# Language-model tower on one core: GpSimd makes the low part of the output weight, and the Fourier update's deltas become stacked float32r products

## The chip, the core and the metric

The kernel is one program on one NeuronCore of a Trainium2 chip. The metric is the device time of one execution in microseconds (us). Engines are named as in the profile: PE is TensorE (PEld its weight loads), DVE is VectorE, ACT is ScalarE, POOL is GpSimd, SP is SyncE, whose queue (SPq) issues almost all DMAs here.

## What is computed

For 2 x 2048 tokens of width 1024:

```python
h = tok_b + sum_k table_k[token at t-3+k]                  # 4 gathered rows
h = h + attention(layernorm(h))                            # 32 heads, 8 kv heads, head 32, causal, RoPE; then @ w_o.T + b_o
base   = x @ W_base.T + b_base                             # x = layernorm(h)
e      = x @ enc.T                                         # enc: 40 rows (32 + 8)
w      = sum_e coefs_e * mask_e                            # [1024, 40]
update = irfft(e @ w.T)                                    # a fixed 1024x1024 orthogonal matrix F
h = h + base + 0.5 * update
```

The kernel folds the update into the weight of the last layer: W1 = W_base.T + enc.T @ (0.5 * w.T @ F). The 40 x 1024 matrix in brackets is called tw in the code; enc.T @ tw, in eight pieces of 128 rows, are the deltas.

## The kernel before

It has three parts, run one after another. Part A (to about 674 us of the span) gathers tokens, normalises and makes queries, keys and values, which go to DRAM as a float32r high part and a low part. Part B (about 676 to 2800 us) is attention without w_o. Part C is the two last matrix products with their layer norm.

Part B works through 16 groups of four heads. Each group has 36 score steps (a 256-query column block c by a 256-key block i, causal) and 164 maxima entries: an entry is one matmul of up to 128 x 512 scores into one of three PSUM banks (L979, with a mask matmul L982 on the diagonal), and one DVE reduction (L918) that gives the row maxima and frees the bank. PE may be three entries ahead of DVE. The maxima run 14 to 18 steps ahead of the scores. A score step is scores (PE, L1017) into PSUM, exp on ACT (L876), and three steps later (LAG) the product with the values on PE (L1035). The softmax denominators are a product with ones (L1052) of a sum of probabilities that POOL adds up first: the 36 steps are put into 20 sets (set_sum, L850 to L858), each set one denominators product. Every order is written out by hand; each engine runs its list strictly in order, and semaphores hold it.

Two other jobs lie inside part B:

- The output weight w_o. In groups 2 to 9 one 128-row piece per group is loaded (w_raw). ACT rounds each half of it to float32r (w0_hi, L888, at steps 8 and 10), and DVE subtracts that from the piece to get the low part (w0_lo, L946, at steps 12 and 14).
- The Fourier update. Before the first scores, PE gives the 66 entries of steps 0 to 13 (`upfront`). Between them stand eight `fourier(c)` (L1087: two float32 matmuls that add up tw in PSUM) and then eight `delta(c)` (L1098: two float32 matmuls, 40 rows deep, into alternating score banks). ACT scales tw (L901) and copies each delta to SBUF (L904), POOL adds it to a base piece (L820), and SP stores the piece (L809). Eight of ten entries after the last delta are what is left of the 66; two belong to step 0 of group 0, whose scores follow.

Of the kernel before, what the change touches and what calls it, by code (L numbers as in the profile page):

```python
# [17 lines left out]
P = 128  # L18
# [548 lines left out]
SET_OF = [j for j, steps in enumerate(SETS) for s in steps]  # L567
LEAD, FIRST_LEAD = 18, 14
TURN_AFTER = 5
FOUR_AT, DELTA_AT = 8, 36  # L570
W_O_GROUP, DEN_GROUP, DEN_PARTS = 2, 11, 8
DEN_COLS = SEQ * HEADS // P // DEN_PARTS
W_IN, EARLY_W1 = 3, 3
# [39 lines left out]
def part_b(nc, hand, w0_hi, w0_lo, q_hi, q_lo, k_hi, k_lo, v_dram, o_dram, den_dram, recip_dram, w_o_t, w_base_t,  # L613
           w1_dram, enc, fourier_t):

    with ExitStack() as ctx:
# [11 lines left out]
        w_raw = sb("w_raw", [P, D], F32)  # L628
        den = w_raw[:, 0:SEQ * HEADS // P]
        with ExitStack() as early:  # L630
            enc_sb, tw = (early.enter_context(nc.sbuf_tensor(n, [R, D], F32)) for n in ("enc_sb", "tw"))
        probs = sb("probs", [P, SLOTS, 2, GROUP, QW], F32)
        sums = sb("sums", [P, SUM_SLOTS, GROUP, QW], F32)
        od_sb = sb("od_sb", [P, 2, 2, QW], F32)
# [9 lines left out]
        v_loaded = [sem(f"v_loaded{c}") for c in range(QC)]  # L644
        ones_done, k_ones_done = sem("ones_done"), sem("k_ones_done")
        enc_in, base_in = sem("enc_in"), [sem(f"base_in{c}") for c in range(DC)]
        tw_ready, tw_done = sem("tw_ready"), sem("tw_done")
        delta_ready, delta_taken = sem("delta_ready"), sem("delta_taken")
        w1_ready, w1_stored = sem("w1_ready"), sem("w1_stored")
        w_raw_in, w0_hi_done, w0_lo_done = sem("w_raw_in"), sem("w0_hi_done"), sem("w0_lo_done")  # L650
# [15 lines left out]
        def _(sp):  # L666
# [54 lines left out]
            def group(g, first, last):  # L721
# [62 lines left out]
                next_v(2)  # L784
                next_v(3)

            for c in range(FOUR_EARLY, DC):
                sp.dma_start(hand.four[c][:], fourier_t[c * P:(c + 1) * P, :]).then_inc(four_in[c], 16)
            sp.dma_start(enc_sb[:], enc).then_inc(enc_in, 16)
            load_q(0, 2)  # L790
            for c in range(2):
                load_base(c)
            for t in range(TPC):
                sp.wait_ge(hand.v_stored[t], 16 * CHUNKS)
            for s in range(2):
# [1 line left out]
            for c in range(QC):  # L797
                load_k(k_score, 0, c, k_score_loaded)
                load_v(0, c)
            for c in range(2, 4):  # L800
                load_base(c)
            load_q(0, 3)
            send_rows(0, 0)
            for c in range(4, DC):
                load_base(c)
            send_rows(0, 1)
            for c in range(DC):
# [5 lines left out]
        @block.gpsimd  # L813
        def _(pool):
            nc.gpsimd.memset(k_score[M_ROW:P, :].bitcast(F32), 1.0).then_inc(k_ones_done, 1)
            pool.wait_ge(k_ones_done, 1)
            for c in range(DC):
                pool.wait_ge(base_in[c], 16)
                pool.wait_ge(delta_taken, c + 1)
                nc.gpsimd.tensor_tensor(hand.base[:, c, :], hand.base[:, c, :], hand.four[c][:], ALU.add  # L820
                                        ).then_inc(w1_ready, 1)

            for t in range(TPC):
                pool.wait_ge(hand.v_stored[t], 16 * CHUNKS)
            for s in range(2):
                pool.wait_ge(hand.rot_stored[s], 16 * CHUNKS * QK_TILES)
            step = Steps(pool, sum_step, 0)

            def probs_of(g, s, k, lo):
                return probs[:, (g * NS + s) % SLOTS, k, :, lo:QW]  # L830

            def exp_waited(g, s, k):
                pool.wait_ge(exp_done, 2 * (g * NS + s) + k + 1)

            def set_sum(g, j):

                q = g * len(SETS) + j
                at = sums[:, q % SUM_SLOTS]
                diagonal = [s for s in SETS[j] if STEPS[s][0] == STEPS[s][1]]
                wide = [(s, k) for s in SETS[j] for k in range(2) if k == 0 or s not in diagonal]  # L840
                if q >= SUM_SLOTS:
                    g_old, j_old = divmod(q - SUM_SLOTS, len(SETS))
                    pool.wait_ge(batch_done, g_old * NS + SETS[j_old][-1] + 1)
                if len(wide) == 1:
                    exp_waited(g, diagonal[0], 1)
                    nc.gpsimd.tensor_tensor(at[:, :, P:QW], probs_of(g, diagonal[0], 0, P),
                                            probs_of(g, diagonal[0], 1, P), ALU.add).then_inc(sum_done, 1)
                    return
                exp_waited(g, *wide[1])
                step.do(nc.gpsimd.tensor_tensor(at, probs_of(g, *wide[0], 0), probs_of(g, *wide[1], 0), ALU.add))  # L850
                exp_waited(g, *wide[2])
                step.do(nc.gpsimd.tensor_tensor(at, at, probs_of(g, *wide[2], 0), ALU.add))  # L852
                if diagonal:
                    lo, last = P, (diagonal[0], 1)
                else:
                    lo, last = 0, wide[3]
                exp_waited(g, *last)
                nc.gpsimd.tensor_tensor(at[:, :, lo:QW], at[:, :, lo:QW], probs_of(g, *last, lo), ALU.add  # L858
                                        ).then_inc(sum_done, 1)

            for g in range(GROUPS):
                for j in range(len(SETS)):
                    set_sum(g, j)

        @block.scalar
        def _(act):

            def exps(g, s, half):
                c, i = STEPS[s]
                n, lo = g * NS + s, P if i == c and half == 1 else 0  # L870
                act.wait_ge(st_ready, 2 * n + half + 1)
                if half == 0 and n >= SLOTS:
                    g_old, s_old = divmod(n - SLOTS, NS)
                    act.wait_ge(batch_done, n - SLOTS + 1)
                    act.wait_ge(sum_done, g_old * len(SETS) + SET_OF[s_old] + 1)
                nc.scalar.activation(probs[:, n % SLOTS, half, :, lo:QW], st_ps[:, half, :, lo:QW], ACT.Exp,  # L876
                                     scale=float(HD) ** -0.5).then_inc(exp_done, 1)

            def take(g, c):
                act.wait_ge(batch_done, g * NS + LAST_OF[c] + 1)  # L880
                if g * QH + c >= 2:
                    act.wait_ge(stored[c % 2], STORE * (g * (QH // 2) + c // 2))
                nc.scalar.copy(od_sb[:, c % 2], od_ps[:]).then_inc(od_copied, 1)

            def weight_high(c, n):
                cols = slice(n * 512, (n + 1) * 512)
                act.wait_ge(w_raw_in, 16 * (c + 1))
                nc.scalar.copy(w0_hi[:, c, cols], w_raw[:, cols]).then_inc(w0_hi_done, 1)  # L888

            def group(g, first, last):  # L890
                for s in range(NS):
                    k = s - LAG - 1
                    if k % NS in LAST_OF and not (first and k < 0):
                        take(g if k >= 0 else g - 1, LAST_OF.index(k % NS))
                    for half in range(2):
                        exps(g, s, half)
                    if 0 <= g - W_O_GROUP < DC and s in (8, 10):
                        weight_high(g - W_O_GROUP, (8, 10).index(s))

            act.wait_ge(tw_ready, DC)  # L900
            nc.scalar.activation(tw[:], slot_ps[0][0:R, :], ACT.Identity, scale=SCALING).then_inc(tw_done, 1)  # L901
            for c in range(DC):
                act.wait_ge(delta_ready, c + 1)
                nc.scalar.copy(hand.four[c][:], slot_ps[(c + 1) % 2]).then_inc(delta_taken, 1)  # L904
            groups(group)
            take(GROUPS - 1, QH - 1)

        @block.vector
        def _(dve):
# [30 lines left out]
                else:  # L940
                    maxima_rows(g, n, which)

            def weight_low(c, n):
                cols = slice(n * 512, (n + 1) * 512)
                dve.wait_ge(w0_hi_done, 2 * c + n + 1)
                nc.vector.tensor_tensor(w0_lo[:, c, cols], w_raw[:, cols], w0_hi[:, c, cols].bitcast(F32), ALU.subtract  # L946
                                        ).then_inc(w0_lo_done, 1)

            def group(g, first, last):
                for s in range(NS):  # L950
                    for more, n in entries_in(s, first, last):
                        take(g + more, n)
                    if 0 <= g - W_O_GROUP < DC and s in (12, 14):
                        weight_low(g - W_O_GROUP, (12, 14).index(s))
                    if g == DEN_GROUP + 1 and s % 4 == 3 and s // 4 < DEN_PARTS:
                        part = den[:, s // 4 * DEN_COLS:(s // 4 + 1) * DEN_COLS]
                        dve.wait_ge(den_loaded, 16)
# [8 lines left out]
        def _(pe):  # L966
# [123 lines left out]

            def delta(c):
                if c == 0:
                    pe.wait_ge(enc_in, 16)
                    pe.wait_ge(tw_done, 1)
                if c >= 2:
                    pe.wait_ge(delta_taken, c - 1)
                for n in range(2):
                    mm = nc.tensor.matmul(slot_ps[(c + 1) % 2][:, n * 512:(n + 1) * 512], enc_sb[:, c * P:(c + 1) * P],  # L1098
                                          tw[:, n * 512:(n + 1) * 512], start=True, stop=True)
                mm.then_inc(delta_ready, 1)  # L1100

            upfront = [n for k in range(FIRST_LEAD) for n in AT_STEP[k]]
            for j, n in enumerate(upfront):
                give(0, n)
                for what, at in ((fourier, FOUR_AT), (delta, DELTA_AT)):
                    c, between = divmod(j - at, 3)
                    if between == 0 and 0 <= c < DC:
                        what(c)
            groups(group)
# [344 lines left out]
```

## Time and profile before

| | us |
|---|---|
| median of 3 runs | 3563.59 |
| lowest, highest | 3561.82, 3579.18 |
| profiled execution, its own time | 3567.09 |
| its span | 3565.3 |
| mean granted TensorE clock | 0.978 of full speed |

The profiled execution is 3.5 us above the median of the runs, and its time is 1.8 us above its span. The clock has two levels, 1.2 and 2.4 GHz; a granted clock of 0.50 is the lower, 1.00 the upper.

### The profile page before, as it was taken

How to read it: one execution, taken by the hardware profiler on the slowest of the kernel's cores; microseconds unless marked ns; L12 is line 12 of the kernel's file. 1: busy time of each engine (PE TensorE's matmuls, PEld its weight loads, DVE VectorE, ACT ScalarE, POOL GpSimd, SP SyncE). 2: the span in 40 equal slices, each digit the busy share in tenths (PEclk: the TensorE clock that was granted, in tenths of full speed). 3: DMA queues.
4: the chain of work that ended last, by engine and by line, in shares of the span. 5: the costliest groups of instructions: out<-in, count | busy, mean ns of one | idle time of the engine just before them, and what ended most of it. 6: DMA issues, size and time to landing. Idle time of an engine off the chain costs nothing. (4 is left out here: it accounts for less than half of the span.)

```text
span 3565.3 us, 61290 instructions
## 1 busy us (share of the span) xinstructions
PE 3413.7 (96%) x25088; PEld 2362.2 (66%) x25088; DVE 2288.3 (64%) x3914; ACT 1421.9 (40%) x1677; POOL 2266.6 (64%) x1042
## 2 busy tenths in 40 slices
PE   1999999999999999999999999999999799999999
PEld 1778888646666566566566666666665488888887
DVE  3677777667777777777777777777775344444443
ACT  2222232135555555555555555555555301111010
POOL 4443220159889889889989989998998622222221
PEclk8999999979999999999999999999999899999999
DMA  8999874721221122122122122112212234333332
GB/s 230 248 255 233 238 207 132 208 77 33 57 62 49 43 64 57 36 62 56 38 68 60 28 61 59 45 42 62 50 39 63 83 88 94 93 90 90 94 95 65
DMA packets 248219, 334.59 MB, mean 94 GB/s; under 512 B 64346, under 2 KB 153818, under 8 KB 247938
## 3 DMA queue, kind: packets, MB, share of 16 engines
q1 hardware_dynamic: 229506, 263.54, 27.3%
q0 software_dynamic: 18432, 67.12, 8.8%
q8 instruction: 198, 3.24, 0.4%
q14 instruction: 83, 0.68, 0.1%
HBM read 227.80 MB, written 101.71 MB: 92 GB/s over the span
## 5 line engine op out<-in xcount | busy, mean ns | idle before, releaser
L918 DVE TENSOR_REDUCE mpart<-mx_ps 128x1 f32<-128x512 f32 (+3 forms) x2560 | 1429.6, 604 | 530.1 <-PE mx_ps L982 342.6
L876 ACT ACTIVATE probs<-st_ps 128x1024 f32<-128x1024 f32 (+1 forms) x1152 | 1063.9, 974 | 828.2 <-PE st_ps L1017 642.7
L979 PE MATMUL mx_ps<-k_max,qs 96*128 96x512 f32 (+3 forms) x2560 | 907.5, 415 | 16.3 <-DVE mpart L918 12.3
L1017 PE MATMUL st_ps<-qs,k_score 98*128 98x512 f32 (+1 forms) x2304 | 719.9, 407 | 0.2
L850 POOL TENSOR_TENSOR sums<-probs 128x1024 f32<-128x1024 f32 x256 | 610.1, 2383 | 160.4 <-ACT probs L876 160.4
L979 PEld LDWEIGHTS mx_ps<-k_max,qs 96*128 96x128 f32 x2560 | 463.9, 194 | 313.1 <-DVE mpart L918 206.1
L852 POOL TENSOR_TENSOR sums<-sums,probs 128x1024 f32<-128x1024 f32 x256 | 609.7, 2381 | 37.8 <-ACT probs L876 19.9
L1035 PE MATMUL od_ps<-probs,vs 128*32 128x256 f32 (+1 forms) x9216 | 595.3, 376 | 0.0
L858 POOL TENSOR_TENSOR sums<-sums,probs 128x1024 f32<-128x1024 f32 (+1 forms) x256 | 543.8, 2124 | 20.3 <-ACT probs L876 0.3
L1017 PEld LDWEIGHTS st_ps<-qs,k_score 98*128 98x128 f32 x2304 | 421.3, 194 | 72.6 <-ACT probs L876 12.3
L1210 POOL TENSOR_TENSOR h<-h,bb 128x1024 f32<-128x1024 f32 x32 | 104.1, 3254 | 509.1 <-DVE xn_c L1284 509.1
L1035 PEld LDWEIGHTS od_ps<-probs,vs 128*32 128x32 f32 x9216 | 242.5, 110 | 229.8 <-issue 116.7
L291 POOL DMA_INDIRECT hbuf<-in_tok_table,idx_all x128 | 193.8, 1514 | 307.2 <-DMA hbuf<-in_tok_table,idx_all 162.5
L491 PE MATMUL qk_ps<-x_hi,w_hi 128*128 128x512 f32 x640 | 254.3, 397 | 17.0 <-ACT rotation L343 14.7
L491 PE MATMUL qk_ps<-x_lo,w_hi 128*128 128x512 f32 x640 | 251.4, 393 | 0.0
L491 PE MATMUL qk_ps<-x_hi,w_lo 128*128 128x512 f32 x640 | 251.4, 393 | 0.0
L982 PE MATMUL mx_ps<-masks 128*128 128x128 bf16 x1024 | 238.0, 234 | 0.0
L1272 DVE TENSOR_TENSOR h<-oc_ps,h_in 128x1024 f32<-128x1024 f32 x31 | 38.0, 1224 | 256.3 <-PE oc_ps L1325 256.3
L1052 PE MATMUL od_ps<-sums,ones 128*32 128x256 f32 (+1 forms) x2560 | 186.0, 363 | 16.1 <-POOL sums L858 16.1
L982 PEld LDWEIGHTS mx_ps<-masks 128*128 128x128 bf16 x1024 | 100.8, 98 | 103.0 <-issue 60.1
L1237 ACT ACTIVATE std_c<-var_c 128x1 f32<-128x1 f32 x32 | 6.5, 203 | 405.2 <-DVE var_c L1279 405.2
L1325 PE MATMUL f_ps<-w_hi,xc_hi 128*128 128x512 f32 x512 | 158.9, 392 | 6.4 <-DVE xc_lo L1294 6.4
(108 smaller groups left out, 4076.5 us busy)
## 6 DMA issues: line engine op xcount, KB each, us to landing
qs<-q_hi_scratch SPq DMA_DIRECT2D x128, 256.0 KB, 4.8
h_scratch<-hbuf SPq DMA_DIRECT2D x32, 512.0 KB, 8.3
q_hi_scratch<-rot_hi SPq DMA_DIRECT2D x64, 256.0 KB, 4.0
q_lo_scratch<-rot_lo SPq DMA_DIRECT2D x64, 256.0 KB, 4.7
qs<-q_lo_scratch SPq DMA_DIRECT2D x64, 256.0 KB, 5.8
o_scratch<-od_sb SPq DMA_DIRECT2D x128, 128.0 KB
o_in<-o_scratch SPq DMA_DIRECT2D x32, 512.0 KB, 5.0
o_in<-recip_scratch SPq DMA_DIRECT2D x128, 128.0 KB, 8.1
```

Source lines behind the costliest of these rows:

```text
L291: nc.gpsimd.indirect_dma_start(hbuf[:, m % 2, t, :], None, tables[k], bass.IndirectOffsetOnAxis(ap=idx[:, m, j:j + 1], axis=0), compute_op ...
L491: mm = nc.tensor.matmul(qk_ps[:, f % 2, :], w[a], x[b], start=(c == 0 and k == 0), stop=(c == DC - 1 and k == 2))
L850: step.do(nc.gpsimd.tensor_tensor(at, probs_of(g, *wide[0], 0), probs_of(g, *wide[1], 0), ALU.add))
L852: step.do(nc.gpsimd.tensor_tensor(at, at, probs_of(g, *wide[2], 0), ALU.add))
L858: nc.gpsimd.tensor_tensor(at[:, :, lo:QW], at[:, :, lo:QW], probs_of(g, *last, lo), ALU.add).then_inc(sum_done, 1)
L876: nc.scalar.activation(probs[:, n % SLOTS, half, :, lo:QW], st_ps[:, half, :, lo:QW], ACT.Exp, scale=float(HD) ** -0.5).then_inc(exp_done, 1)
L918: nc.vector.tensor_reduce(mpart[:, h * TPC + t, kc:kc + 1], mx_ps[:, e % MAX_BANKS, 0:w], AX, ALU.max).then_inc(max_done, 1)
L979: mm = nc.tensor.matmul(out, qs[c][0:K_ROWS, h, t * P:(t + 1) * P], k_max[0:K_ROWS, kc * CT:kc * CT + w], start=True, stop=not diagonal)
L982: mm = nc.tensor.matmul(out[:, w - P:w], ident_m, mqk, start=False, stop=True)
L1017: mm = nc.tensor.matmul(out[:, :, lo:QW], k_score[0:M_ROW + 2, kt * P:(kt + 1) * P], qs[c // 2][0:M_ROW + 2, h:h + 2, at + lo:at + QW], st ...
L1035: mm = nc.tensor.matmul(od_ps[h * HD:(h + 1) * HD, 0, lo:QW], vs[:, 2 * i + k, :], probs[:, n % SLOTS, k, h, lo:QW], start=s in FIRST_OF a ...
L1052: mm = nc.tensor.matmul(od_ps[h * HD:(h + 1) * HD, 1, lo:QW], ones[:], sums[:, q % SUM_SLOTS, h, lo:QW], start=False, stop=s in LAST_OF)
```

## The change

1. `weight_low` leaves DVE's list and enters POOL's, with the same 16 operations (128 x 512, two SBUF inputs), now after sets 7 and 10 of a group.
2. `delta` uses float32r. The exact float32 product of two 40-row operands is replaced by one float32r product 120 rows deep: enc3 holds high, high and low rows of enc, and tw3 high, low and high rows of tw. The low parts are made on POOL (enc_lo, tw_lo), the high parts on ACT, and four small DMAs on SP's queue (`rows_sent`) copy the second and third 40 rows to their partitions.
3. A fourier stands after every second entry from entry 8 (before: every third), so the last is at entry 22 (before: 29). A delta stands after every entry from entry 50 (before: every third from 36). The last delta is at entry 57 in both.
4. On SP's queue enc is loaded first, one base piece is loaded early and seven after the tw rows.

```diff
-FOUR_AT, DELTA_AT = 8, 36
+FOUR_AT, FOUR_EVERY, DELTA_AT, DELTA_EVERY = 8, 2, 50, 1
@@ SP
+            def rows_sent(dst, row, src, sent):
+                sp.dma_start(dst[row:row + R].bitcast(F32), src[0:R].bitcast(F32)).then_inc(sent, 16)
+
+            sp.dma_start(enc_sb[:], enc).then_inc(enc_in, 16)
             for c in range(FOUR_EARLY, DC):
                 sp.dma_start(hand.four[c][:], fourier_t[c * P:(c + 1) * P, :]).then_inc(four_in[c], 16)
-            sp.dma_start(enc_sb[:], enc).then_inc(enc_in, 16)
             load_q(0, 2)
-            for c in range(2):
-                load_base(c)
+            sp.wait_ge(enc_hi_done, 1)
+            rows_sent(enc3, R, enc3, enc_rows)
+            sp.wait_ge(enc_lo_done, 1)
+            rows_sent(enc3, 2 * R, enc_lo, enc_rows)
+            load_base(0)
...
-            for c in range(2, 4):
-                load_base(c)
             load_q(0, 3)
             send_rows(0, 0)
-            for c in range(4, DC):
+            sp.wait_ge(tw_hi_done, 1)
+            rows_sent(tw3, 2 * R, tw3, tw_rows)
+            sp.wait_ge(tw_lo_done, 1)
+            rows_sent(tw3, R, tw_lo, tw_rows)
+            for c in range(1, DC):
                 load_base(c)
@@ POOL
+            nc.gpsimd.tensor_tensor(enc_lo[:], enc_sb[:], enc3[0:R].bitcast(F32), ALU.subtract).then_inc(enc_lo_done, 1)
...
+            nc.gpsimd.tensor_tensor(tw_lo[:], tw[:], tw3[0:R].bitcast(F32), ALU.subtract).then_inc(tw_lo_done, 1)
...
+            def weight_low(c, n):
+                cols = slice(n * 512, (n + 1) * 512)
+                pool.wait_ge(w0_hi_done, 2 * c + n + 1)
+                nc.gpsimd.tensor_tensor(w0_lo[:, c, cols], w_raw[:, cols], w0_hi[:, c, cols].bitcast(F32), ALU.subtract
+                                        ).then_inc(w0_lo_done, 1)
+
             for g in range(GROUPS):
                 for j in range(len(SETS)):
                     set_sum(g, j)
+                    if 0 <= g - W_O_GROUP < DC and j in (7, 10):
+                        weight_low(g - W_O_GROUP, (7, 10).index(j))
@@ ACT
+            act.wait_ge(enc_in, 16)
+            nc.scalar.copy(enc3[0:R], enc_sb[:]).then_inc(enc_hi_done, 1)
             act.wait_ge(tw_ready, DC)
+            nc.scalar.activation(tw3[0:R], slot_ps[0][0:R, :], ACT.Identity, scale=SCALING).then_inc(tw_hi_done, 1)
             nc.scalar.activation(tw[:], slot_ps[0][0:R, :], ACT.Identity, scale=SCALING).then_inc(tw_done, 1)
@@ DVE
-            def weight_low(c, n):
...
-                    if 0 <= g - W_O_GROUP < DC and s in (12, 14):
-                        weight_low(g - W_O_GROUP, (12, 14).index(s))
@@ PE
                 if c == 0:
-                    pe.wait_ge(enc_in, 16)
-                    pe.wait_ge(tw_done, 1)
+                    pe.wait_ge(enc_rows, 32)
+                    pe.wait_ge(tw_rows, 32)
...
-                    mm = nc.tensor.matmul(slot_ps[(c + 1) % 2][:, n * 512:(n + 1) * 512], enc_sb[:, c * P:(c + 1) * P],
-                                          tw[:, n * 512:(n + 1) * 512], start=True, stop=True)
+                    mm = nc.tensor.matmul(slot_ps[(c + 1) % 2][:, n * 512:(n + 1) * 512], enc3[:, c * P:(c + 1) * P],
+                                          tw3[:, n * 512:(n + 1) * 512], start=True, stop=True)
...
-                for what, at in ((fourier, FOUR_AT), (delta, DELTA_AT)):
-                    c, between = divmod(j - at, 3)
+                for what, at, every in ((fourier, FOUR_AT, FOUR_EVERY), (delta, DELTA_AT, DELTA_EVERY)):
+                    c, between = divmod(j - at, every)
```

On PE, the end of the upfront list stood like this before (mx_ps rows are maxima entries, L1098 a delta, L1017 the first scores):

```order
L979 MATMUL mx_ps<-k_max,qs 128x512 x3
L1098 MATMUL st_ps<-tw,enc_sb 128x512 x2
L979 MATMUL mx_ps<-k_max,qs 128x512 x2
L987 MATMUL mx_ps<-ident,mcol 16x128
L1098 MATMUL st_ps<-tw,enc_sb 128x512 x2
L979 MATMUL mx_ps<-k_max,qs 128x512 x3
L1098 MATMUL st_ps<-tw,enc_sb 128x512 x2
L979 MATMUL mx_ps<-k_max,qs 128x512 x10
L1017 MATMUL st_ps<-qs,k_score 128x512
```

and stands like this now (L1121 is a delta, L1040 the first scores):

```order
L1121 MATMUL st_ps<-tw,enc 128x512 x2
L1010 MATMUL mx_ps<-ident,mcol 16x128
L1121 MATMUL st_ps<-tw,enc 128x512 x2
L1002 MATMUL mx_ps<-k_max,qs 128x512
L1121 MATMUL st_ps<-tw,enc 128x512 x2
L1002 MATMUL mx_ps<-k_max,qs 128x512
L1121 MATMUL st_ps<-tw,enc 128x512 x2
L1002 MATMUL mx_ps<-k_max,qs 128x512
L1121 MATMUL st_ps<-tw,enc 128x512 x2
L1002 MATMUL mx_ps<-k_max,qs 128x512 x10
L1040 MATMUL st_ps<-qs,k_score 128x512
```

The deltas have one entry between them where they had three, and the ten entries behind the last one are the same. Ahead of them, 28 entries now follow the last fourier without any other product.

On DVE, in group 2, the two low parts stood between reductions of step 12 to 14 (x41 and x9 are reductions in a row):

```order
L931 TENSOR_SCALAR m_hi<-mx_ps 16x128
L933 SCALAR_TENSOR_TENSOR m_lo<-mx_ps,m_hi 16x128
L918 TENSOR_REDUCE mpart<-mx_ps 128x1 x41
L946 TENSOR_TENSOR w_lo<-w_raw,w_hi 128x512
L918 TENSOR_REDUCE mpart<-mx_ps 128x1 x9
L946 TENSOR_TENSOR w_lo<-w_raw,w_hi 128x512
L918 TENSOR_REDUCE mpart<-mx_ps 128x1 x9
L922 TENSOR_REDUCE mcol<-mpart 128x16
```

On POOL in the same group they now stand behind the sums of sets 7 and 10 (each set is three additions, L870 to L878):

```order
L878 TENSOR_TENSOR sums<-sums,probs 128x1024
L884 TENSOR_TENSOR w_lo<-w_raw,w_hi 128x512
L870 TENSOR_TENSOR sums<-probs 128x1024
L872 TENSOR_TENSOR sums<-sums,probs 128x1024
L878 TENSOR_TENSOR sums<-sums,probs 128x1024
L870 TENSOR_TENSOR sums<-probs 128x1024
L872 TENSOR_TENSOR sums<-sums,probs 128x1024
L878 TENSOR_TENSOR sums<-sums,probs 128x4x128
L870 TENSOR_TENSOR sums<-probs 128x1024
L872 TENSOR_TENSOR sums<-sums,probs 128x1024
L878 TENSOR_TENSOR sums<-sums,probs 128x1024
L884 TENSOR_TENSOR w_lo<-w_raw,w_hi 128x512
```

DVE's list in a group with a weight piece is now the same as in one without; POOL's is longer by two operations.

## Rows read from the trace of the kernel before

**Rows 1.** The page: span, and busy time of the engines.

```profile
span 3565.3 us, 61290 instructions
PE 3413.7 (96%) x25088; PEld 2362.2 (66%) x25088; DVE 2288.3 (64%) x3914; ACT 1421.9 (40%) x1677; POOL 2266.6 (64%) x1042
```

**Rows 2.** Timeline of ACT, copies of finished column blocks: start us, us, engine, line.

```profile
1029.13 0.59 ACT L883 COPY od_sb<-od_ps 128x512 f32<-128x512 f32 x1 [0.93 <-PE od_ps L1052]
...
1316.68 0.59 ACT L883 COPY od_sb<-od_ps 128x512 f32<-128x512 f32 x1 [0.45 <-PE od_ps L1052]
1337.34 0.59 ACT L883 COPY od_sb<-od_ps 128x512 f32<-128x512 f32 x1
...
2064.20 0.59 ACT L883 COPY od_sb<-od_ps 128x512 f32<-128x512 f32 x1 [0.93 <-PE od_ps L1052]
2190.20 0.59 ACT L883 COPY od_sb<-od_ps 128x512 f32<-128x512 f32 x1 [0.93 <-PE od_ps L1052]
...
2221.28 0.59 ACT L883 COPY od_sb<-od_ps 128x512 f32<-128x512 f32 x1 [0.45 <-PE od_ps L1052]
2238.10 0.59 ACT L883 COPY od_sb<-od_ps 128x512 f32<-128x512 f32 x1
```

**Rows 3.** Instructions of L946: duration ns min/median/max, first and last start us.

```profile
L946 DVE TENSOR_TENSOR w_lo<-w_raw,w_hi x16: 2416/2603/2769, 1059.7 to 1974.3; 128x512 fp32r<-128x512 f32 x16
```

**Rows 4.** Timeline of DVE, POOL and ACT, group 2; first row part A.

```profile
672.79 0.68 DVE L433 TENSOR_TENSOR rot_lo<-rotation,rot_hi 128x512 fp32r<-128x512 f32 x1
...
1059.73 2.42 DVE L946 TENSOR_TENSOR w_lo<-w_raw,w_hi 128x512 fp32r<-128x512 f32 x1
...
1059.22 2.38 POOL L852 TENSOR_TENSOR sums<-sums,probs 128x1024 f32<-128x1024 f32 x1
...
1052.17 0.62 ACT L888 CAST w_hi<-w_raw 128x512 fp32r<-128x512 f32 x1
```

**Rows 5.** Timeline of POOL and PE, group 11 (no weight piece).

```profile
2234.45 2.38 POOL L850 TENSOR_TENSOR sums<-probs 128x1024 f32<-128x1024 f32 x1 [2.11 <-ACT probs L876]
...
2252.79 2.39 POOL L858 TENSOR_TENSOR sums<-sums,probs 128x1024 f32<-128x1024 f32 x1
...
2258.81 0.61 PE L1052 MATMUL od_ps<-sums,ones 128*32 128x256 f32 x8
```

**Rows 6.** Timeline of PE, start of part B.

```profile
679.42 3.17 PE L1087 MATMUL st_ps<-four,wr 128*40 128x512 f32 x4
...
694.11 0.72 PE L979 MATMUL mx_ps<-k_max,qs 96*128 96x512 f32 x2
694.76 1.91 PE L1087 MATMUL st_ps<-four,wr 128*40 128x512 f32 x4
...
742.26 3.78 PE L1098 MATMUL st_ps<-tw,enc_sb 40*128 40x512 f32 x4
745.97 5.95 PE L979 MATMUL mx_ps<-k_max,qs 96*128 96x512 f32 x10
751.72 0.63 PE L1017 MATMUL st_ps<-qs,k_score 98*128 98x512 f32 x1
...
768.01 0.40 PE L1052 MATMUL od_ps<-sums,ones 128*32 128x128 f32 x8
```

**Rows 7.** Windows: stretch, length, busy PE, PEld, DVE, ACT, POOL, then clock, DMA share.

```profile
706.00:760.00 54.00, 54.00 (x99) 23.33 (x97) 22.56 (x40) 12.63 (x13) 20.01 (x9) 0.50 0.34 123
```

**Rows 8.** Timeline of DVE, ACT, POOL, start of part B.

```profile
746.80 6.07 DVE L918 TENSOR_REDUCE mpart<-mx_ps 128x1 f32<-128x512 f32 x10 [3.40 <-PE mx_ps L979]
...
702.17 1.02 ACT L901 ACTIVATE tw<-st_ps 40x1024 f32<-40x1024 f32 x1 [29.58 <-PE st_ps L1087]
...
747.23 2.36 POOL L820 TENSOR_TENSOR base<-base,four 128x1024 f32<-128x1024 f32 x1 [2.95 <-ACT four L904]
...
755.39 1.27 POOL L846 TENSOR_TENSOR sums<-probs 128x512 f32<-128x512 f32 x1 [5.80 <-ACT probs L876]
```

**Rows 9.** Instructions on base: landing of its DMAs, eight loads and eight stores.

```profile
DMA to landing us min/median/max: 2.9/5.0/15.2
```

More of the change, by code:

```diff
@@ L630, in part_b @@
         with ExitStack() as early:
-            enc_sb, tw = (early.enter_context(nc.sbuf_tensor(n, [R, D], F32)) for n in ("enc_sb", "tw"))
+            held = lambda n, rows, d: early.enter_context(nc.sbuf_tensor(n, [rows, D], d))
+            enc_sb, tw = held("enc_sb", R, F32), held("tw", R, F32)
+            enc_lo, tw_lo = held("enc_lo", R, F32R), held("tw_lo", R, F32R)
+            enc3, tw3 = held("enc3", 3 * R, F32R), held("tw3", 3 * R, F32R)
         probs = sb("probs", [P, SLOTS, 2, GROUP, QW], F32)
@@ L646, in part_b @@
         enc_in, base_in = sem("enc_in"), [sem(f"base_in{c}") for c in range(DC)]
-        tw_ready, tw_done = sem("tw_ready"), sem("tw_done")
+        enc_hi_done, enc_lo_done, enc_rows = sem("enc_hi_done"), sem("enc_lo_done"), sem("enc_rows")
+        tw_ready, tw_done, tw_hi_done = sem("tw_ready"), sem("tw_done"), sem("tw_hi_done")
+        tw_lo_done, tw_rows = sem("tw_lo_done"), sem("tw_rows")
         delta_ready, delta_taken = sem("delta_ready"), sem("delta_taken")
@@ L816, in _ @@
             pool.wait_ge(k_ones_done, 1)
+            pool.wait_ge(enc_hi_done, 1)
+            nc.gpsimd.tensor_tensor(enc_lo[:], enc_sb[:], enc3[0:R].bitcast(F32), ALU.subtract).then_inc(enc_lo_done, 1)
+            pool.wait_ge(enc_lo_done, 1)
+            pool.wait_ge(tw_hi_done, 1)
+            pool.wait_ge(tw_done, 1)
+            nc.gpsimd.tensor_tensor(tw_lo[:], tw[:], tw3[0:R].bitcast(F32), ALU.subtract).then_inc(tw_lo_done, 1)
+            pool.wait_ge(tw_lo_done, 1)
             for c in range(DC):
@@ L941, in take @@
                     maxima_rows(g, n, which)
-            def weight_low(c, n):
[L944 to L947, printed above, removed]
             def group(g, first, last):
```

## The prediction

> **What bounds the kernel now.** I read the page first: PE is busy for 96% of the span, DVE and POOL for 64% each [rows 1]. PE sets the pace, so an edit is worth what it takes out of PE's waits or off PE's own list, wherever it stands. Two stretches concern the change.
>
> The first is attention. Each group ends its first column block with a copy on ACT, so the distance between two such copies is a group's length. The reader is to see two lengths. From group 2 to group 10 it is 2064.20 - 1029.13 = 1035.07 us for eight groups, 129.4 each; from there to group 11 it is 126.00 [rows 2]. Only groups 2 to 9 hold a weight piece. Inside a group the difference sits in one place: between the copies of blocks 3 and 4 lie 20.66 us in group 4 and 16.82 us in group 11, so 3.84 of it [rows 2]. That is where DVE does its two low parts. Each takes 2.4 to 2.8 us, 16 in all [rows 3], while the same form in part A takes 0.68 [rows 4]. The first of them starts at 1059.73 and ends at 1062.15; POOL's addition, begun at 1059.22, ends at 1061.60 [rows 4]. What is left behind POOL's end is 0.55 us, about the length of the operation. So DVE stands and waits until POOL's instruction is over. Three maxima banks cover 1.8 us of reductions, and PE then stands too.
>
> That wait has a rule in the Trainium skill (SBUF — State Buffer, "Who interferes with whom"): a DVE operation with two SBUF inputs and a GpSimd operation take one shared port pair exclusively, and the later one blocks. The trace agrees: 1061.60 plus 0.55 is DVE's end.
>
> The second stretch is the start of part B, 679.42 (first fourier) to 751.72 (first scores). The last delta ends at 745.97 [rows 6]. PE never rests there, and from 706 to 760 it has the lower clock, 0.50 or 1.2 GHz [rows 7]. A float32 delta takes 3.71 us of it (742.26 to 745.97) [rows 6].
>
> **The weight's low part leaves DVE.** DVE's list in groups 2 to 9 becomes that of group 11, so each should take 126.00: 1035.07 - 8 x 126.00 = **27.1 us** less. ACT's two roundings stay; group 2's second is at 1052.17, before the disputed stretch, and delayed nothing there.
>
> **It enters POOL.** No row shows this form on POOL. The nearest is its addition of 128 x 512, 1.27 us [rows 8]; the upper bound is one of twice the size, 2.39 [rows 5]; the lower is DVE's 0.68 [rows 4]. I take 1.27, the same element count. What does it delay? In group 11 POOL waits 2.11 us for ACT before set 9 [rows 5], so the operation behind set 7 is absorbed there. Behind set 10 there is no such gap at once: set 11 is summed at 2255.18 and PE asks for it at 2258.81, 3.63 us later [rows 5]. 1.27 fits, 2.39 too. Sets 12 to 15 come with the same delay, until the next wait for ACT. Both inputs are old by then (ACT rounds at steps 8 and 10, set 7 ends with step 12). Cost 0; if that cover were gone, 16 x 1.27 = 20 us. SP's next load of w_raw waits for the low parts, but only at the next group's start.
>
> The Trainium skill speaks against this edit (GPSIMD Engine Reference, "Engine selection"): two-input elementwise work belongs on VectorE, GpSimd being about 2x slower. The rows give 1.27 against 0.68, so by engine time alone 16 x 0.59 = 9 us would be lost where I count 27 gained. The traced DVE time, 2.6, is the one that counts here.
>
> **Fouriers closer.** Product and cost stay: the first at the low clock ends at 682.6, each later one takes 1.84 (1.91 less 0.07 overlap), two entries 0.65 [rows 6]. So the last ends at 682.6 + 7 x 2.49 = 700.0, where before ACT began tw at 702.17 [rows 8]: 2.1 us earlier.
>
> **From there to the first delta.** 28 entries, nothing else. DVE sets their pace: 6.07 / 10 = 0.61 for a wide one [rows 8]. The 16 diagonal ones are narrower; before, 28 entries and 8 deltas filled 702.2 to 745.97, so 43.8 - 8 x 3.71 = 14.1, 0.50 an entry. I take 12 x 0.61 + 16 x 0.50 = 15.3, less two entries (1.2) that PE is ahead: first delta at about 714.1.
>
> **Are the tw rows there?** ACT makes tw3 and tw, 1.02 each [rows 8], to 702.1. POOL's tw_lo over 40 x 1024 has no row; its 128 x 1024 operation takes 2.36 [rows 8], and one partition's length is the same: 704.5. Its DMA then lands within 2.9 to 15.2 us, the quickest and slowest on base (stores in an idle queue, loads in a full one), median 5.0 [rows 9]. Only one base load now stands ahead, three fewer, so I take the median: 709.5, with 4.6 us of slack. At 15.2 it is 719.7 and PE waits 5.6. The enc rows go 15 us earlier and cost nothing; SP comes to the key loads about 2 us later, but those keys are first used at the scores. The four loads sit one 160 KB load later; the six had landed well before use and I charge nothing, at most 1 us.
>
> **Deltas.** Each is two matmuls of 512 columns in one float32r pass, at 1.2 GHz 0.43 us each: 0.86 for 3.71. An entry between costs PE 0.43. 8 x 0.86 + 7 x 0.43 = 9.9: the last ends at 724.0. ACT's copy, about as long as tw's 1.02, frees the bank two deltas later, at 2.6 us, so it does not hold. Behind the last delta the same ten entries as before: 751.72 - 745.97 = 5.75. First scores at 729.8, **21.9 us** earlier.
>
> **What is late next.** POOL's eight additions to base, 2.36 each [rows 8], 18.9 in all, now start at about 716.4 and end at 735.3. POOL took up the first sum at 755.39 [rows 8], shifted to 733.5: 1.8 us late. PE asked for it at 768.01 [rows 6], 11.4 us after its end, so nothing waits. SP stands in the stores as long; its next work, group 1's queries, waits for the scores of step 2 anyway.
>
> **Sum.** 27.1 + 21.9 = 49.0. The profiled execution goes from 3567.1 to 3518.1. The median is 3.5 lower than that execution: 3563.6 - 49.0 = **3514.6**.
>
> **The rivals.**
>
> *The rows come late* (or another wait of that size at the first delta). For: four DMAs in a queue whose loads took up to 15.2. Against: 3 base loads fewer ahead. Loses 5.6: 3520. Chance 0.12.
>
> *POOL's operation costs more than its slack.* It must pass 3.6 us behind set 10. At twice the upper bound, 4.8, PE loses 1.2 us, eight times: 10 us, 3524. Chance 0.06.
>
> *It was not the low parts but the rest of the weight work* (ACT's roundings, the load). Then groups stay at 129.4 and only 21.9 comes: 3542. Against it: the delay begins behind block 3's copy. Chance 0.04. If half of each gain is lost by something unseen, 3539, also here.
>
> *Price by engine time* (the rule above): 3563.6 - 21.9 + 9 gives 3551, no change that can be told. As a mechanism: POOL is the bound in the weight groups, and each operation there shows in full. Against it: POOL's 2.11 us wait for ACT. Chance 0.02.
>
> *Slower.* POOL's operation would have to block until PE loses more than is gained: with 3.6 us of slack behind set 10 and 5 behind set 7, 16 operations must take some 49.0 / 16 + 4.3 = 7.4 us each to reach no change, and 8.5 for 0.5% slower, at least three and a half times the upper bound. Chance 0.01.
>
> **How the numbers follow.** Forecast 0.75, 3514.6. Its own spread: the clock. If it rises earlier, because the deltas are dense and 120 rows deep, the deltas and first steps cost up to 7 us less; if it rises later, 3 more. Narrow entries between 0.40 and 0.60 are 1.6 either way. With the late rows and the costlier POOL operation inside, 3506 to 3528. 0.5% (18 us) is about what a measurement of this kernel can tell; the border for faster is 3545.8. Faster 0.96, same 0.03, slower 0.01.
>
> **What would show it.** Right: all 15 distances between group copies at 126.0 (group 0 apart); low parts on POOL at about 1.3 us; no DVE row of 2.4; first scores near 730 and first delta near 714 with no idle time on PE for a DMA. Wrong: a wait of denominators (L1052's counterpart) for POOL sums behind sets 8 or 11; PE idle at the first delta; groups 2 to 9 still longer than 126.

## The result, and the profile after

The changed kernel takes 3514.97 us (median of 4 runs, 3510.39 to 3517.75); beside it the kernel before took 3562.70 (4 runs, 3559.94 to 3579.18). The difference of the medians is 47.7 us. The ratio of the runs is 0.9853, 95% interval 0.9836 to 0.987 (it is not the quotient of the two medians, which is 0.9866): 1.5% faster, at the predicted time and inside its range. The profiled execution took 3517.54 us, with a span of 3515.7, 49.6 less than before.

The page of the changed kernel, busy times:

```profile
PE 3374.0 (96%) x25072; PEld 2349.4 (67%) x25072; DVE 2251.6 (64%) x3898; ACT 1422.5 (40%) x1679; POOL 2289.2 (65%) x1060
```

The shares read as those of before [rows 1]; one cannot see in them where 50 us went. The group lengths can. Timeline of ACT, the copies that answer to [rows 2] (start us, us, engine, line):

```profile
1008.96 0.59 ACT L911 COPY od_sb<-od_ps 128x512 f32<-128x512 f32 x1 [0.93 <-PE od_ps L1075]
...
1292.05 0.59 ACT L911 COPY od_sb<-od_ps 128x512 f32<-128x512 f32 x1 [0.45 <-PE od_ps L1075]
1308.86 0.58 ACT L911 COPY od_sb<-od_ps 128x512 f32<-128x512 f32 x1
...
2016.99 0.59 ACT L911 COPY od_sb<-od_ps 128x512 f32<-128x512 f32 x1 [0.93 <-PE od_ps L1075]
2142.96 0.59 ACT L911 COPY od_sb<-od_ps 128x512 f32<-128x512 f32 x1 [0.93 <-PE od_ps L1075]
```

Groups 2 to 9 take 2016.99 - 1008.96 = 1008.03 us, 126.0 each, like the group after them (125.97). That is 27.04 less than 1035.07. In group 4 the copies of blocks 3 and 4 are 16.81 us apart, where they were 20.66 apart.

The low parts, and POOL's timeline around the first of them in group 2:

```profile
L884 POOL TENSOR_TENSOR w_lo<-w_raw,w_hi x16: 1269/1284/1293, 1043.8 to 1948.7; 128x512 fp32r<-128x512 f32 x16
```

```profile
1043.83 1.29 POOL L884 TENSOR_TENSOR w_lo<-w_raw,w_hi 128x512 fp32r<-128x512 f32 x1
1045.09 2.37 POOL L870 TENSOR_TENSOR sums<-probs 128x1024 f32<-128x1024 f32 x1
...
1053.22 2.38 POOL L870 TENSOR_TENSOR sums<-probs 128x1024 f32<-128x1024 f32 x1 [0.84 <-ACT probs L904]
```

An operation takes 1.28 us on POOL where it took 2.6 on DVE. Before set 9 POOL now waits 0.84 us for ACT, 1.27 less than the 2.11 in [rows 5]: the wait has swallowed the operation.

The other gain is at the start of part B. Timeline of PE (an x8 groups eight instructions that follow each other):

```profile
678.54 0.30 PE L1002 MATMUL mx_ps<-k_max,qs 96*128 96x128 f32 x1 [2.57 <-PEq L158]
...
682.21 3.64 PE L1110 MATMUL st_ps<-four,wr 128*40 128x512 f32 x4
...
701.80 1.91 PE L1110 MATMUL st_ps<-four,wr 128*40 128x512 f32 x4
703.64 0.97 PE L1002 MATMUL mx_ps<-k_max,qs 96*128 96x512 f32 x3
...
718.74 1.05 PE L1121 MATMUL st_ps<-tw,enc 120*128 120x512 f32 x2
719.59 0.63 PE L1002 MATMUL mx_ps<-k_max,qs 96*128 96x512 f32 x1
720.02 1.05 PE L1121 MATMUL st_ps<-tw,enc 120*128 120x512 f32 x2
...
726.46 0.73 PE L1121 MATMUL st_ps<-tw,enc 120*128 120x512 f32 x2
727.03 0.85 PE L1002 MATMUL mx_ps<-k_max,qs 96*128 96x512 f32 x3
...
732.14 0.39 PE L1040 MATMUL st_ps<-qs,k_score 98*128 98x512 f32 x1
```

From the first maxima matmul to the first scores it is 732.14 - 678.54 = 53.6 us; before, the scores at 751.72 [rows 6] stood 75.31 behind their first maxima matmul (676.41). That is 21.7 less. No delta waits for its rows. The granted clock by stretch (the columns of [rows 7]; the clock is the third number from the end):

```profile
710.00:718.00 8.00, 8.00 (x31) 5.41 (x30) 7.13 (x16) 0.00 (x0) 0.00 (x0) 0.50 0.94 353
718.00:726.00 8.00, 7.80 (x22) 5.32 (x23) 5.81 (x12) 5.48 (x6) 4.99 (x3) 0.67 0.29 116
726.00:740.00 14.00, 12.79 (x46) 6.27 (x44) 13.55 (x23) 7.57 (x9) 14.00 (x7) 1.00 0.65 263
...
742.00:746.00 4.00, 4.00 (x18) 2.89 (x17) 1.40 (x5) 1.82 (x2) 3.65 (x3) 0.50 0.53 117
```

It is low when the deltas begin and back at 1.00 before they end; before, it stayed at 0.50 up to 760. But it is low once more from about 740 to 747, behind the first scores. The first copy of a column block stands 16.2 us behind the first scores here. In three of the experiments below that start in the same way, the clock stays at 1.00 in that stretch, and it is 13.7. So about 2.5 us of the start vary between executions of the same order.

The two gains make 48.7 of the span's 49.6. The rest is small differences with both signs: part A 2.1 us longer, the stretch from the first scores to the first copy 0.6 shorter, the last group with part C 2.4 shorter. The change touches neither part A nor part C, and in the other kernels the first maxima matmul stands anywhere from 674.8 to 680.8.

### The profile page after: what moved, and what is told of

Its sections match the earlier page's. It is cut to its first block and busy times, and to the rows that moved or that the text cites. A ratio compares the mean times of both kernels' runs of the same rounds, so it can differ in the third digit from the quotient of the medians.

```text
span 3515.7 us, 61268 instructions
## 1 busy us (share of the span) xinstructions
PE 3374.0 (96%) x25072; PEld 2349.4 (67%) x25072; DVE 2251.6 (64%) x3898; ACT 1422.5 (40%) x1679; POOL 2289.2 (65%) x1060
## 5 line engine op out<-in xcount | busy, mean ns | idle before, releaser
L1040 PE MATMUL st_ps<-qs,k_score 98*128 98x512 f32 (+1 forms) x2304 | 720.4, 408 | 0.2
L870 POOL TENSOR_TENSOR sums<-probs 128x1024 f32<-128x1024 f32 x256 | 609.7, 2382 | 128.8 <-ACT probs L904 128.0
L878 POOL TENSOR_TENSOR sums<-sums,probs 128x1024 f32<-128x1024 f32 (+1 forms) x256 | 538.8, 2105 | 20.3 <-ACT probs L904 0.3
L1040 PEld LDWEIGHTS st_ps<-qs,k_score 98*128 98x128 f32 x2304 | 421.2, 194 | 73.0 <-ACT probs L904 12.4
```

Of the source, the lines that this page charges most:

```text
L1040: mm = nc.tensor.matmul(out[:, :, lo:QW], k_score[0:M_ROW + 2, kt * P:(kt + 1) * P], qs[c // 2][0:M_ROW + 2, h:h + 2, at + lo:at + QW], st ...
```

## The experiments

The theory is that of the prediction: DVE's subtraction waits for the port that it shares with POOL, POOL has room for the work, and the start is what the deltas cost at the low clock. The rivals: the weight groups were long for another reason; POOL has no room; the order of the products, not their form, gave the start. Each kernel is the changed one but for its edit, except the second, which is the kernel before. "Less" is the difference of the medians of the kernel before and of the experiment, on the same chip (three sets of runs; before 3566.84 for the first four, 3568.62 for the next four and 3569.34 for the last two). Group lengths, the start (first maxima matmul to first scores) and the distance from the same matmul to the first copy of a column block are from the profiled execution, in us. In the kernels that have the changed one's order there the start spreads from 52.2 to 53.6 and the first copy from 65.9 to 69.8; in the kernel before they are 75.3 and 92.1.

| kernel | median us | less | ratio (95%) | groups 2 to 9 | start of part B | to the first copy |
|---|---|---|---|---|---|---|
| low part on DVE | 3541.21 | 25.6 | 0.9929 (0.9912 to 0.9945) | 128.2 to 129.9 | 53.3 | 67.0 |
| only the low part moved | 3541.25 | 25.6 | 0.993 (0.9914 to 0.9947) | 126.0 | 76.2 | 95.8 |
| low part twice | 3512.69 | 54.2 | 0.9852 (0.9835 to 0.9868) | 126.0 | 52.2 | 65.9 |
| low part four times | 3572.91 | -6.1 | 1.0013 (1.0004 to 1.0023) | 133.1 to 133.6 | 53.6 | 69.8 |
| DVE reads the piece alone | 3512.96 | 55.7 | 0.9847 (0.983 to 0.9863) | 126.0 to 126.1 | 53.3 | 67.0 |
| float32 deltas | 3542.36 | 26.3 | 0.9932 (0.9915 to 0.9949) | 126.0 to 126.1 | 80.1 | 96.9 |
| old places | 3522.13 | 46.5 | 0.9867 (0.9847 to 0.9888) | 126.0 to 126.1 | 56.6 | 76.2 |
| fouriers every third | 3511.22 | 57.4 | 0.9847 (0.9828 to 0.9867) | 126.0 | 50.2 | 63.9 |
| products spread | 3519.97 | 49.4 | 0.986 (0.9845 to 0.9875) | 126.0 | 54.7 | 69.8 |
| deltas every second | 3512.87 | 56.5 | 0.9837 (0.9824 to 0.9851) | 125.9 to 126.0 | 50.3 | 66.6 |

**The two halves.** The first kernel gives the low part back to DVE, the second makes only that move in the kernel before.

```diff
 # low part on DVE: the changed kernel
-                    if 0 <= g - W_O_GROUP < DC and j in (7, 10):      # POOL
-                        weight_low(g - W_O_GROUP, (7, 10).index(j))
...
+                    if 0 <= g - W_O_GROUP < DC and s in (12, 14):     # DVE
+                        weight_low(g - W_O_GROUP, (12, 14).index(s))
```

The function `weight_low` moves with its calls, and `nc.gpsimd` in it becomes `nc.vector`.

> The changed kernel with the weight's low part back on DVE at steps 12 and 14; the start of part B stays changed. Wait theory (DVE stands until POOL's running instruction is over, PE then runs out of maxima banks): groups 2 and 3 at 128.2, groups 4 to 9 at 129.8 again, 27 us more than the changed kernel, 3542. Rival (the weight groups are long because of ACT's roundings or the load): nothing returns, 3515. Rival (the two parts of the change hide one another): clearly more or less than 27.

> The kernel before with only the move of the low part to POOL. If the two terms simply add: 27 us less than before, 3536, all groups at 126.0 and the start of part B as before (first scores 75.3 us after part B's first matmul). Rival (the terms are coupled, for instance POOL's backlog at the start matters): another number than 27.

In the first the low parts are slow again, with everything else as changed:

```profile
L969 DVE TENSOR_TENSOR w_lo<-w_raw,w_hi x16: 2406/2587/2773, 1036.4 to 1949.8; 128x512 fp32r<-128x512 f32 x16
```

Its weight groups are 128.2 to 129.9, in the second all are 126.0. By ratio the halves give 0.7% each, 1.4% together, against 1.47% for the whole, each with an interval of about 0.17% on either side: within that they add up, and nothing is seen to be given back between them.

**Twice and four times.** POOL repeats the same subtraction.

```diff
+                for k in range(3):                                    # 1 for twice
+                    step.do(nc.gpsimd.tensor_tensor(w0_lo[:, c, cols], w_raw[:, cols], w0_hi[:, c, cols].bitcast(F32),
+                                                    ALU.subtract))
                 nc.gpsimd.tensor_tensor(w0_lo[:, c, cols], w_raw[:, cols], w0_hi[:, c, cols].bitcast(F32), ALU.subtract
                                         ).then_inc(w0_lo_done, 1)
```

> The changed kernel with each low-part operation on POOL made twice (the same values are written twice; 1.28 us more, 1.35 with the hand-over). Slack theory: behind set 10 the changed kernel has 2.39 us left between POOL's sum of set 11 and PE's use. Twice costs about 0.6 behind set 7 after the wait for ACT, and 1.35 behind set 10, so 0.4 us is left: groups stay at 126.0 and the time at 3515. Rival (POOL is the bound in these groups and each operation shows): 16 x 1.35 = 22 us more, 3537.

> The changed kernel with each low-part operation on POOL made four times (same values). Slack theory: 4 x 1.35 = 5.4 us behind set 7, of which some 2.1 is absorbed in POOL's wait for ACT, so 3.3 late at set 9, against a slack of 3.47; then 5.4 more behind set 10 against 3.6: PE waits some 5 us in each of eight groups, about 40 us more, 3555 (30 to 50). POOL-bound rival: 48 x 1.35 = 65 us more, 3580.

Twice costs nothing. Four times costs 7.2 us in each of the eight groups, some 58 in all, where the slacks of the prediction gave 40 (30 to 50): a miss. In size that is nearer to the 65 of the rival by which every operation on POOL shows in full; what speaks against this rival is twice, where it wanted 22 us and none came. Four times, timeline of POOL and of PE in group 3, and PE's denominators in the weight groups (busy us, mean ns, idle before and its releaser):

```profile
1205.58 4.01 POOL L885 TENSOR_TENSOR w_lo<-w_raw,w_hi 128x512 fp32r<-128x512 f32 x3
1209.67 1.28 POOL L887 TENSOR_TENSOR w_lo<-w_raw,w_hi 128x512 fp32r<-128x512 f32 x1
1210.91 2.38 POOL L870 TENSOR_TENSOR sums<-probs 128x1024 f32<-128x1024 f32 x1
...
1218.18 1.08 PE L1078 MATMUL od_ps<-sums,ones 128*32 128x256 f32 x8 [4.31 <-POOL sums L878]
```

```profile
L1078 PE MATMUL od_ps<-sums,ones 128*32 128x256 f32 (+1 forms) x1160 | 86.3, 371 | 31.2 <-POOL sums L878 30.2
```

Two things were missing in my slacks. The two places share one budget: what the operation behind set 7 costs beyond POOL's 2.11 us of waiting is still there behind set 10. So 2 x 5.14 - 2.11 - 3.63 = 4.5 us, and 4.31 is measured; with 5.33, the time from 1205.58 to the next sum at 1210.91, it would be 4.9. For twice, 2 x 2.57 - 5.74 is below zero. And the clock falls with the idle time. The same kernel, windows behind that wait:

```profile
1216.00:1218.00 2.00, 0.00 (x0) 0.00 (x0) 0.00 (x0) 0.00 (x0) 2.00 (x1) 0.75 0.00 0
1218.00:1220.00 2.00, 1.81 (x10) 0.91 (x11) 0.00 (x0) 0.58 (x1) 2.00 (x3) 0.50 0.00 0
1220.00:1222.00 2.00, 2.00 (x6) 1.52 (x6) 1.29 (x2) 0.69 (x1) 1.92 (x2) 0.50 0.20 68
```

31.2 us of waits in the window of 1043 to 2015 are about 4 a group; the other 3 go with PE at 0.50 for some 5 us behind each. That this halving costs 3 is argued from the rows, not tried by itself.

**DVE reads the piece alone.** If DVE waited for its SBUF operands as such, and not for a port that only two inputs need, any DVE operation on the piece at these steps would wait.

```diff
+                    if 0 <= g - W_O_GROUP < DC and s in (12, 14):     # DVE, POOL keeps the low part
+                        half = (12, 14).index(s)
+                        dve.wait_ge(w0_hi_done, 2 * (g - W_O_GROUP) + half + 1)
+                        nc.vector.tensor_reduce(scrap[:], w_raw[:, half * 512:(half + 1) * 512], AX, ALU.max
+                                                ).then_inc(scrap_done, 1)
```

SP's next load of the piece waits for `scrap_done` too (not shown).

> The changed kernel with two more operations on DVE in groups 2 to 9, at steps 12 and 14 where the low parts stood: a maximum over one half of w_raw, 128 x 512 from SBUF, one input, about 0.6 to 0.7 us of engine time, the same as a low part's own. The low parts stay on POOL. Port theory (only a DVE operation with two SBUF inputs waits for POOL's instruction): each shows as 0.6 to 0.7 us, is mostly covered by the three banks, groups at 126.0 to 126.6, at most 5 us in all, 3515 to 3520. Rival (any extra DVE work or any SBUF input there costs the same): DVE rows of 2.4 us and groups at 128 to 130, 3542.

```profile
L985 DVE TENSOR_REDUCE scrap<-w_raw x16: 673/676/677, 1033.6 to 1922.3; 128x1 f32<-128x512 f32 x16
```

Timeline of the same kernel, the first of them and POOL's operation at that time:

```profile
1033.60 0.68 DVE L985 TENSOR_REDUCE scrap<-w_raw 128x1 f32<-128x512 f32 x1
...
1033.05 2.39 POOL L876 TENSOR_TENSOR sums<-sums,probs 128x1024 f32<-128x1024 f32 x1
```

It begins and ends inside POOL's addition and takes 0.68 us; all 16 do. The wait belongs to an operation of DVE with two SBUF inputs while POOL has one that reads SBUF, as the Trainium skill says (SBUF — State Buffer, "Who interferes with whom").

A reduction is not a subtraction: it also writes one column where the subtraction writes 512. Four things support the reading. The two-input form too takes 0.68 while POOL has no addition to make [rows 4]. Before the change all 16 subtractions ended 0.55 or 0.56 us behind the end of POOL's running addition. The next addition of POOL was the longer one then, 2.68 or 2.69 for 2.38, which fits each engine waiting for the other. And a DVE operation that writes 64 columns, but has one SBUF input, does not wait either: the kernel before has eight such reciprocals in group 12, all beside an addition of POOL, at 541 to 545 ns. Kernel before, POOL behind the first low part, and the third reciprocal:

```profile
1061.68 2.68 POOL L858 TENSOR_TENSOR sums<-sums,probs 128x1024 f32<-128x1024 f32 x1
...
2343.89 0.54 DVE L958 RECIPROCAL w_raw<-w_raw 128x64 f32<-128x64 f32 x1
...
2343.82 2.39 POOL L850 TENSOR_TENSOR sums<-probs 128x1024 f32<-128x1024 f32 x1
```

No run has an operation with one input that writes all 512 columns there.

**Float32 deltas.** The stacked operands are still made, but the product is the old one.

```diff
-                    mm = nc.tensor.matmul(slot_ps[(c + 1) % 2][:, n * 512:(n + 1) * 512], enc3[:, c * P:(c + 1) * P],
-                                          tw3[:, n * 512:(n + 1) * 512], start=True, stop=True)
+                    mm = nc.tensor.matmul(slot_ps[(c + 1) % 2][:, n * 512:(n + 1) * 512], enc_sb[:, c * P:(c + 1) * P],
+                                          tw[:, n * 512:(n + 1) * 512], start=True, stop=True)
```

> The changed kernel with float32 deltas, 40 rows deep, at the new places (all preparation of the stacked operands stays and is waited for). Forecast's term: a float32 delta costs 3.7 us at 1.2 GHz against 0.86, so eight cost 23 us more, from 53.6 to about 76 us between part B's first matmul and the first scores, 3538. Rival (the gain came from the places, since the entries between the old deltas were hidden work): a few us only, about 3520. With the clock at 2.4 GHz in the deltas it would be 8 x 1.85 = 15 against 8.7, 6 to 8 us more.

```profile
715.17 3.78 PE L1121 MATMUL st_ps<-tw,enc_sb 40*128 40x512 f32 x4
719.61 3.78 PE L1121 MATMUL st_ps<-tw,enc_sb 40*128 40x512 f32 x4
```

With the new places and the old product the start is 80.1 us, longer than before the change. The form of the product is worth 26.5 us against the changed kernel's start, all of the gain and more; the medians say 29.4 against DVE reads the piece alone, measured beside it (3542.36 and 3512.96). The eight deltas stand 4.43 apart and take 34.3 us where the changed kernel takes 8.3, and the clock is at 0.50 from 706 to 760. How much of this is the shorter product and how much the clock that comes back earlier was not separated; at the low clock alone a delta with its entry takes 4.43 against 1.28.

**The places.** `FOUR_AT, FOUR_EVERY, DELTA_AT, DELTA_EVERY` is 8, 2, 50, 1 in the changed kernel.

```diff
-FOUR_AT, FOUR_EVERY, DELTA_AT, DELTA_EVERY = 8, 2, 50, 1
+FOUR_AT, FOUR_EVERY, DELTA_AT, DELTA_EVERY = 8, 3, 36, 3   # old places
+FOUR_AT, FOUR_EVERY, DELTA_AT, DELTA_EVERY = 8, 3, 50, 1   # fouriers every third
+FOUR_AT, FOUR_EVERY, DELTA_AT, DELTA_EVERY = 2, 3, 40, 2   # products spread
+FOUR_AT, FOUR_EVERY, DELTA_AT, DELTA_EVERY = 8, 3, 44, 2   # deltas every second
```

> The changed kernel with float32r deltas at the old places (fouriers every third entry from 8, deltas every third from 36). The last fourier is at entry 29, six entries before the first delta; the stacked rows land some 8 us after the last fourier, so PE should wait at the first delta for about 5 us, and the rest of the entries are the same work: first scores about 3 us later than in the changed kernel, 3518. Rival (places do not matter): 3515. Rival (the wait also lowers the clock for the deltas and costs more): 3522.

> The changed kernel with the fouriers every third entry (8 to 29) and the deltas still every entry from 50. Three entries take DVE 1.8 us, as long as a fourier takes PE, so DVE's idle time of the changed kernel between fouriers is filled: the last fourier ends 0.6 us later, with 7 entries fewer behind it (4.2 us). 3.6 us less than the changed kernel, 3511, first scores 50 us after part B's first matmul; the stacked rows must land within 21 entries (11 us), which leaves 3. Rival (the rows are late): no gain, 3515.

> Only the numbers that place the products differ from the changed kernel: Fourier products from entry 2 at every third entry, delta products from entry 40 at every second. If the part between the first maxima and the first scores is set by the sum of PE's work and by its clock, the products filling gaps that DVE's reductions leave, this start is 2 to 4 us shorter than the changed kernel's 53.6 us and the time is some 3 us less, hardly to be told from it. If the rows of the second product have to be in place first, as in the kernel with the products at their old places (it waited 4.6 us), PE waits up to 5 us at the first delta and the time is not below that of the changed kernel.

> Fourier products from entry 8 at every third, deltas from entry 44 at every second. The first delta comes some 2.5 us later in the entries than in the kernel with the products spread furthest, so the rows are there and PE waits for none of them; the start is 2 to 4 us shorter than the changed kernel's 53.6 us. If a denser row of deltas is what raises the clock, it stays at the low level here and the start is as long as the changed kernel's or longer.

The first delta at the old places, and then with the products spread:

```profile
714.71 1.19 PE L1121 MATMUL st_ps<-tw,enc 120*128 120x512 f32 x2 [4.56 <-DMA tw<-tw_lo]
```

```profile
713.54 1.19 PE L1121 MATMUL st_ps<-tw,enc 120*128 120x512 f32 x2 [1.99 <-DMA tw<-tw_lo]
```

So the rows can be late, and a later first delta is what hides them. With the old places the cost is larger than this wait. The clock is 0.50 from 714 to 726 and low again behind it (0.57 from 734 to 746), so the first copy comes 9.2 us later than in DVE reads the piece alone, and the medians of these two, measured side by side, are 9.2 apart as well. That is the rival of its expectation by which the wait lowers the clock; that the wait is what lowers it is argued. The rows leave POOL at 711.6 and 707.3 in these two, and land 3.1 and 6.2 us later; with deltas every second it is 3.1 again and a wait of 0.9, where none was expected. The densest fouriers gain nothing: one after every third entry gives the shortest start, 50.2. More entries then stand beside the fouriers: DVE is busy for 8.9 of the 12 us from 690 to 702, in the changed kernel for 5.8. Against the changed kernel's 53.6 that is 3.4 us, against the shortest start of the same order 2.0, and the medians cannot tell them apart (1.7 us less than DVE reads the piece alone beside it; 0.9847 and 0.9853, each interval 0.003 to 0.004 wide). Deltas at every second entry end at the same start, with the clock back at 1.00 as well, so the clock does not need a delta after every entry to come back; there group 0 is 2.8 us longer than in the changed kernel (137.44 against 134.61, at a clock of 0.98), which eats most of the gain in the profiled execution. No version beats the changed kernel by what can be measured.

## Why the prediction was right, step by step

The mechanism of both gains is borne out, but for the closer fouriers. That the time came within 0.4 us of the forecast is luck: the changed kernel's own runs spread over 7 us, two kernels with the same start and the same group lengths (low part twice, DVE reads the piece alone) gave 54.2 and 55.7 us in their sets where 49.0 was forecast, and two errors at the start cancelled (below).

- **The low part leaves DVE, 27.1 us.** Measured 27.04, and shown by both halves. Its mechanism was half of the story: groups 2 and 3 were 2.2 us too long, groups 4 to 9 3.8 (below).
- **It enters POOL at no cost.** Shown, by the groups of 126.0 and by the low part twice. The price of 1.27 was 1.28. The two slacks were used as if they were separate; at this size that did not matter. It did in the rival called slower: its break-even of 7.4 us an operation is wrong, since four operations in a row, about 5.2 us, already end at 1.0013. The rival stood nearer than it was put, but still four times the real price off.
- **Fouriers closer, the last one 2.1 us earlier.** The weakest step. Counted from the first maxima matmul the last fourier ended after 25.1 us, forecast 23.6: the first one ran wholly at the low clock (3.64 us, before 3.17), and the entries around it too. The entries up to the first delta took 15.1 for 14.1; with the clock at 0.50 the widest diagonal ones stand 0.67 us apart, where 0.50 was taken for all 16. Together the first delta is 2.5 us late, and the experiment with the old distance shows that the closer fouriers bring nothing: its start is, if anything, 2.0 to 3.4 us shorter.
- **The rows.** Landing 5.0 was assumed; 3.1 to 6.2 is what the other places show. In the changed kernel POOL is done with them at 708.2 and the first delta begins at 718.7. By those landings the room was 4.3 to 7.4 us, forecast 4.6; the landing itself is not in its rows.
- **Deltas and the ten entries behind, 9.9 and 5.75 us.** Measured 8.3 and 5.1. At the low clock a delta with its entry takes 1.28, forecast 1.29; the clock then rose within the eight, which stood only in the spread. These 2.3 us made up for the 2.5 lost ahead, so that 21.7 against 21.9 is closer than its parts were. At the high clock one delta did wait for ACT's copy, by 0.20 us, which was put at nothing. That the clock would fall once more behind the first scores stood nowhere; it lies outside the 21.7.
- **Late next: POOL.** Its base additions end at 739.7, where the first sum begins; forecast 735.3, to which part A's 2.1 us and the late first delta are to be added. PE did not wait for it.
- **Price by engine time.** Refuted: it came to 9 us lost, and the kernel that makes only this move gained 25.6. The rule of the Trainium skill (GPSIMD Engine Reference, "Engine selection") compares the engines alone, and there the rows agree with its factor of about 2 (1.28 against 0.68). Beside a busy POOL the DVE operation takes 2.6.
- **The signs.** The distances between group copies are 125.97 to 126.13 behind group 0, 14 of them and not 15 as written. The first delta stood at 718.74 for 714 and the first scores at 732.14 for 730; 2.1 us of both is the longer part A.

## What to carry to other kernels

An operation of DVE that lasts four times as long as its own form elsewhere may be waiting inside the instruction: look at what POOL runs at its end, and price the move by the traced duration, not by the engine's speed. When work goes to an engine with gaps, count its gaps as one budget from the insertion to the next consumer, and double the work once in an experiment to see how near the edge is. At this start, with PE at its low clock, the form of a product was worth far more (26.5 us) than its place between other instructions (2 to 4 us), as long as PE did not wait for operands.

## What the runs showed of the hardware

Short idle times can cost PE more than their length, but do not always. Before the change PE stood for the DVE low part equally long in groups 2 and 4. Timeline of PE in the kernel before:

```profile
1062.80 0.33 PE L979 MATMUL mx_ps<-k_max,qs 96*128 96x128 f32 x1 [0.88 <-DVE mpart L918]
...
1319.27 0.33 PE L979 MATMUL mx_ps<-k_max,qs 96*128 96x128 f32 x1 [0.87 <-DVE mpart L918]
```

Windows of the kernel before, behind each:

```profile
1064.00:1066.00 2.00, 2.00 (x39) 1.59 (x32) 0.73 (x3) 0.00 (x0) 2.00 (x2) 1.00 0.03 11
...
1321.00:1323.00 2.00, 2.00 (x31) 1.62 (x23) 0.00 (x0) 0.00 (x0) 2.00 (x1) 0.50 0.04 10
```

In group 4 the granted clock fell to 0.50 for some 3.5 us, in group 2 it stayed at 1.00. That goes with group lengths of about 128.2 (groups 2 and 3) against 129.8 (groups 4 to 9), and so with some 9 of the 27 us; the same two lengths came back with the low part on DVE (groups 2 to 4 at 128.2 to 128.3, groups 5 to 9 at 129.7 to 129.9), one group later. What decides in which group it begins to fall stays open.

DVE and POOL also hold each other up in part C, where both work on two SBUF inputs. Timeline of DVE and POOL in the kernel before:

```profile
2926.40 1.22 DVE L1258 TENSOR_TENSOR a_f<-o_in 128x1024 f32<-128x1024 f32 x1
2928.74 2.22 DVE L1262 TENSOR_TENSOR a_lo<-a_f,a_hi 128x1024 fp32r<-128x1024 f32 x1 [1.12 <-ACT a_hi L1219]
...
2926.57 3.31 POOL L1210 TENSOR_TENSOR h<-h,bb 128x1024 f32<-128x1024 f32 x1 [16.04 <-DVE xn_c L1284]
2929.84 3.37 POOL L1206 TENSOR_TENSOR h_in<-h_in,bo 128x1024 f32<-128x1024 f32 x1
```

DVE's operation that began first takes 1.22, and POOL's behind it 3.31 where its addition of that size takes 2.38 elsewhere. Then the order turns: DVE's next one begins inside POOL's and takes 2.22, ending 1.08 us behind it, and POOL's second one again takes about 1 us more. The one that begins first is not held up, whichever engine it is on.
